# Transposes three steps and values four steps behind the scores in a fused attention and FFN kernel

## The reference

```python
x = x + 0.5 * ffn(layernorm(x))
x = x + attention(layernorm(x))
x = x + 0.5 * ffn(layernorm(x))

# attention: 16 heads of 64
h = silu(x @ W1.T + b1) @ W2.T + b2
q, k, v = split(h @ Wg.T + bg)
dots = q @ k.T * 64 ** -0.5
dots = where(j >= i + 64, -inf, dots)      # token i sees j < i + 64
out = softmax(dots) @ v
return out.reshape(b, n, 1024) @ Wo.T + bo
# ffn: silu(x wg) * (x wu) @ wd, hidden 384, weights from integers
```

## Time and profile before

| | |
|---|---|
| median of 3 runs | 1632.81 us (1631.20 to 1634.49) |
| profiled execution, time | 1628.43 us |
| its span | 1626.6 us |
| TensorE busy | 1439.0 us, 88% |
| GpSimd busy | 990.7 us, 61% |
| VectorE busy | 970.6 us, 60% |
| ScalarE busy | 776.3 us, 48% |
| mean granted TensorE clock | 0.976 of full |

### The profile page before, as it was taken

How to read it: one execution, slowest core, us unless ns; L and a number is a source line. 1 busy time by engine, 2 the same in 40 slices (tenths; PEclk the granted TensorE clock), 3 DMA queues, 4 the chain that set the end, 5 groups by cost and what they waited for, 6 DMA issues and landing times.

```text
span 1626.6 us, 38540 instructions
## 1 busy us (share of the span) xinstructions
PE 1439.0 (88%) x13330; PEld 1113.7 (68%) x13330; DVE 970.6 (60%) x1886; ACT 776.3 (48%) x1827; POOL 990.7 (61%) x592
## 2 busy tenths in 40 slices
PE   4767999999999999999999999999999999998676
PEld 3543777777777777777777777777777777777566
DVE  5653666666666666566666656666666656665444
ACT  2323555555555455554555555555555455454332
POOL 2231767677666667666676766677666666667410
PEclk9995999999999999999999999999999999999978
DMA  3100000000000000000000000000000000000000
GB/s 96 36 0 18 19 19 19 18 18 18 18 18 18 13 5 18 18 18 18 18 18 18 18 18 18 18 18 18 18 18 18 18 1 17 18 0 1 1 26 26
DMA packets 30571, 29.42 MB, mean 18 GB/s; under 512 B 6993, under 2 KB 25298, under 8 KB 30546
## 3 DMA queue, kind: packets, MB, share of 16 engines
q1 hardware_dynamic: 30546, 29.09, 5.9%
HBM read 8.07 MB, written 2.10 MB: 6 GB/s over the span
## 4 chain that ended last, share of the span: by engine, by line
PE 55%; issue 17%; DVE 13%; POOL 7%; ACT 6%; DVEq 1%; DMA 1%; ACTq 0%; POOLq 0%; SPq 0%
PE banks L773 16%; PE banks L754 15%; PE banks L789 8%; PE banks L719 6%; POOL probs L324 6%; ACT probs L389 5%; DVE probst L549 4%; DVE negmax L537 4%; PE banks L655 4%; PE banks L742 2%; PE banks L723 2%; DVE hidden L492 1%; PE banks L734 1%; POOL rstd_ln L295 1%; DVE xn_ln L478 1%
## 5 line engine op out<-in xcount | busy, mean ns | idle before, releaser
L324 POOL TENSOR_SCALAR probs<-probs,recips 128x704 f32<-128x704 f32 (+7 forms) x512 | 947.6, 1864 | 452.5 <-DVE recips L542 452.5
L537 DVE TENSOR_REDUCE negmax<-banks 128x1 f32<-128x704 f32 (+7 forms) x512 | 392.6, 808 | 129.8 <-PE banks L754 129.8
L773 PE MATMUL banks<-ident,probs 128*128 128x128 f32 x2752 | 391.4, 281 | 43.2 <-DVE probst L549 22.6
L397 ACT ACTIVATE probst<-banks 128x512 f32<-128x512 f32 (+1 forms) x320 | 177.4, 555 | 516.2 <-PE banks L773 516.2
L389 ACT ACTIVATE probs<-banks,negmax 128x704 f32<-128x704 f32 (+7 forms) x512 | 397.2, 785 | 44.5 <-DVE negmax L537 44.5
L773 PEld LDWEIGHTS banks<-ident,probs 128*128 128x128 f32 x2752 | 293.2, 141 | 130.3 <-issue 69.3
L549 DVE COPY probst<-banks 128x512 f32<-128x512 f32 (+1 forms) x416 | 276.6, 665 | 171.8 <-PE banks L773 169.8
L789 PE MATMUL banks<-probst,vs 128*64 128x128 f32 x5504 | 357.0, 277 | 0.8 <-ACT probst L397 0.8
L789 PEld LDWEIGHTS banks<-probst,vs 128*64 128x64 f32 x5504 | 295.3, 137 | 37.6 <-issue 22.5
L754 PE MATMUL banks<-kt,qt 64*128 64x512 f32 (+4 forms) x2496 | 298.3, 365 | 3.1 <-issue 3.1
L754 PEld LDWEIGHTS banks<-kt,qt 64*128 64x128 f32 x2496 | 206.0, 186 | 50.5 <-issue 5.8
(11 more groups left out here) (58 smaller groups left out, 881.1 us busy)
## 6 DMA issues: line engine op xcount, KB each, us to landing
hslot<-h_sb SPq DMA_DIRECT2D x32, 512.0 KB, 3.2
wslot<-in_wqkvt SPq DMA_DIRECT2D x32, 128.0 KB, 3.0
wslot<-wq_sb SPq DMA_DIRECT2D x32, 64.0 KB, 2.6
y<-xres SPq DMA_DIRECT2D x8, 256.0 KB, 2.3
wo_sb<-in_wot SPq DMA_DIRECT2D x1, 512.0 KB
wq_sb<-in_wqkvt SPq DMA_DIRECT2D x1, 512.0 KB
bslot<-bqk_sb SPq DMA_DIRECT2D x32, 1.0 KB, 1.9
iload<-in_wgatet SPq DMA_DIRECT2D x1, 192.0 KB, 2.4
```

Source lines behind the costliest of these rows:

```text
L324: nc.gpsimd.tensor_scalar(here, here, recips[:, c, h:h + 1], None, ALU.mult).then_inc(normed.sem, 1)
L397: nc.scalar.activation(probst[c % 2][:, 4 * g:4 * g + w, :].rearrange("p t q -> p (t q)"), banks[:, TRANSPOSED[g % 2], 0:w * P], ACT.Copy) ...
L537: nc.vector.tensor_reduce(negmax[:, c, h:h + 1], src, AX.X, ALU.max, negate=True).then_inc(maxed.sem, 1)
L773: last = nc.tensor.transpose(banks[:, TRANSPOSED[g % 2], (t - 4 * g) * P:(t - 4 * g + 1) * P], probs[c, h][:, kb * P:(kb + 1) * P], ident[:])
```

## The change

`T_LAG` goes from 2 to 3 and `PV_LAG` from 3 to 4. In step 0 the transposes are now those of step 5's tile of the turn before and the values those of step 4's.

`JOBS` is spread anew. The k and q jobs go to steps 4 to 7. v0 and v1 go to steps 1 and 3 and are now those of the turn itself, no longer of the next. An output product o1 now is that of the turn before. Where a step has two jobs (4: o3, k0; 6: o0, k1) the first is an output.

On TensorE a step is now: scores, values, transposes of groups 0 and 1, the first job, groups 2 and 3, the other jobs, masks of the next step. On ScalarE the exponentials come first, the copy of group 1 behind them. On VectorE the reciprocal stands ahead of all jobs and of the copy of group 2. `evict` is the first or second part of a step's jobs there.

Ahead of the first turn v0 and v1 aren't projected any more; behind the last one the drain has four steps instead of three, and three outputs instead of two.

```diff
--- before.py
+++ after.py
@@ -53,13 +53,15 @@
     width = [min(c * P + P + WINDOW, N) for c in range(STEPS)]
     blocks = [-(-w // P) for w in width]
     groups = [-(-2 * n // 4) for n in blocks]
-    T_LAG, PV_LAG = 2, 3
+    T_LAG, PV_LAG = 3, 4
     HEADS = "AB"
     SCORE = (0, 2)
     TRANSPOSED = (4, 5)
     ATTEND = 6
     MISC = 7
-    JOBS = {0: ["k0"], 1: ["o2", "q0"], 2: ["k1"], 3: ["o3", "q1"], 4: ["v0"], 5: ["o0"], 6: ["v1"], 7: ["o1"]}
+    JOBS = {0: ["o1"], 1: ["v0"], 2: ["o2"], 3: ["v1"], 4: ["o3", "k0"], 5: ["q0"], 6: ["o0", "k1"], 7: ["q1"]}
     JOB_ORDER = [(c, job) for c in range(STEPS) for job in JOBS[c]]
     T_BANK = {"ln1": 1, "ln2": 7}
...
@@ -214,9 +216,12 @@
             return (i, c - lag) if c >= lag else (i - 1, c - lag + STEPS)
-        def job_turn(job, c, i):
-            return i + 1 if job[0] in "kqv" else i - 1 if job in ("o2", "o3") else i
+        def job_turn(job, i):
+            return i + 1 if job[0] in "kq" else i - 1 if job in ("o1", "o2", "o3") else i
+        def runs(job, carry, more):
+            return more if job[0] in "kq" else carry or job[0] == "v" or job == "o0"
         block = ctx.enter_context(nc.Block())
...
@@ -403,23 +408,21 @@
                 act.wait_ge(wo_done.sem, wo_done.after(f"o{c // 2}", i - 1))
                 nc.scalar.activation(attn[:, c, :], banks[:, ATTEND, 0:P], ACT.Copy).then_inc(attn_out.sem, 1)
-            def step(c, i, r, carry=True, here=True, more=True):
+            def step(c, i, r, carry=True, more=True):
                 ti, tc = back(i, c, T_LAG)
                 ai, ac = back(i, c, PV_LAG)
-                turning = c < STEPS + T_LAG and (carry or c >= T_LAG)
+                turning = carry or c >= T_LAG
+                exps(c, i)
                 if turning and groups[tc] > 1:
                     take(tc, 1, ti)
-                if here:
-                    exps(c, i)
                 if carry or c >= PV_LAG:
                     attention_out(ac, ai)
                 if turning and groups[tc] > 3:
                     take(tc, 3, ti)
-                if more:
-                    for job in JOBS[c]:
-                        if job[0] in "kq":
-                            queries_keys(job, i + 1, 1 - r)
+                for job in JOBS[c]:
+                    if job[0] in "kq" and more:
+                        queries_keys(job, i + 1, 1 - r)
             for name in qk_high.events:
                 queries_keys(name, 0, 0)
...
@@ -578,24 +580,29 @@
                 ti, tc = back(i, c, T_LAG)
                 turning = carry or c >= T_LAG
                 row_max(c, i)
-                if turning:
+                if turning and groups[tc] > 0:
                     take(tc, 0, ti)
-                for job in JOBS[c]:
-                    if job[0] == "o" and (carry or job in ("o0", "o1")):
-                        add_output(job, job_turn(job, c, i))
+                invert(c, i)
+                for job in JOBS[c][:1]:
+                    evict(job, i, r, carry, more)
                 if turning and groups[tc] > 2:
                     take(tc, 2, ti)
-                invert(c, i)
-                for job in JOBS[c]:
-                    if job[0] == "v" and more:
-                        values(job, i + 1, 1 - r)
-                    if job[0] in "kq" and more:
-                        queries_keys_low(job, i + 1, 1 - r)
+                for job in JOBS[c][1:]:
+                    evict(job, i, r, carry, more)
+            def evict(job, i, r, carry, more):
+                if not runs(job, carry, more):
+                    return
+                if job[0] == "o":
+                    add_output(job, job_turn(job, i))
+                elif job[0] == "v":
+                    values(job, i, r)
+                else:
+                    queries_keys_low(job, i + 1, 1 - r)
             for name in qk_done.events:
                 queries_keys_low(name, 0, 0)
-            values("v0", 0, 0)
-            values("v1", 0, 0)
             for c in range(STEPS):
                 step(c, 0, 0, carry=False)
             with dve.Fori(0, TURNS // 2 - 1) as i2:
...
@@ -608,9 +615,10 @@
             for c in range(T_LAG):
                 ti, tc = back(TURNS, c, T_LAG)
                 take(tc, 0, ti)
-                take(tc, 2, ti)
-            add_output("o2", TURNS - 1)
-            add_output("o3", TURNS - 1)
+                if groups[tc] > 2:
+                    take(tc, 2, ti)
+            for name in ("o1", "o2", "o3"):
+                add_output(name, TURNS - 1)
             dve.wait_ge(wo_added.sem, wo_added.after("o3", TURNS - 1))
             statistics(pd, "ln1", 0, 0)
...
@@ -776,8 +784,8 @@
             def attend(c, i, r):
-                if c == 0:
-                    pe.wait_ge(v_done.sem, v_done.after("v1", i))
+                pe.wait_ge(v_done.sem, v_done.after("v0" if blocks[c] <= 4 else "v1", i))
                 n, s = back(i, c, 1)
                 pe.wait_ge(attn_out.sem, attn_out.after(s, n))
                 for e in range(2):
...
@@ -801,35 +809,29 @@
                 ai, ac = back(i, c, PV_LAG)
                 turning, attending = carry or c >= T_LAG, carry or c >= PV_LAG
-                def runs(job):
-                    return more if job[0] in "kqv" else carry or job in ("o0", "o1")
                 def do(job):
-                    if not runs(job):
+                    if not runs(job, carry, more):
                         return
                     k = JOB_ORDER.index((c, job))
-                    earlier = [(s, name, i) for s, name in JOB_ORDER[:k] if runs(name)]
-                    s, name, t = earlier[-1] if earlier else (*JOB_ORDER[-1], i - 1)
-                    misc_read(name, job_turn(name, s, t))
-                    n = job_turn(job, c, i)
-                    if job[0] in "kqv":
-                        project(job, n, 1 - r)
+                    earlier = [(name, i) for _, name in JOB_ORDER[:k] if runs(name, carry, more)]
+                    name, t = earlier[-1] if earlier else (JOB_ORDER[-1][1], i - 1)
+                    misc_read(name, job_turn(name, t))
+                    n = job_turn(job, i)
+                    if job[0] == "o":
+                        output(job, n)
                     else:
-                        output(job, n)
+                        project(job, n, r if job[0] == "v" else 1 - r)
                 score(c, i, r)
-                if turning:
-                    turns_of(tc, ti, (0, 1))
-                for job in JOBS[c]:
-                    if job[0] == "o":
-                        do(job)
                 if attending:
                     attend(ac, ai, r if c >= PV_LAG else 1 - r)
                 if turning:
+                    turns_of(tc, ti, (0, 1))
+                do(JOBS[c][0])
+                if turning:
                     turns_of(tc, ti, (2, 3))
-                for job in JOBS[c]:
-                    if job[0] != "o":
-                        do(job)
+                for job in JOBS[c][1:]:
+                    do(job)
                 if not (final and c == STEPS - 1):
                     n, s = (i, c + 1) if c + 1 < STEPS else (i + 1, 0)
                     masks(s, n)
...
@@ -838,7 +840,7 @@
             pe.wait_ge(pa.x1.sem, pa.x1.after("x", CHUNKS - 1))
             pe.wait_ge(zeroed, 2 * sum(width[c] < blocks[c] * P for c in range(STEPS)))
             last = None
-            for name in proj.events:
+            for name in ("k0", "q0", "k1", "q1"):
                 if last:
                     misc_read(last, 0)
                 project(name, 0, 0)
...
@@ -862,6 +864,8 @@
                 attend(ac, ai, 1)
                 if c < T_LAG:
                     turns_of(tc, ti, (2, 3))
+            misc_read("o0", TURNS - 1)
+            output("o1", TURNS - 1)
             misc_read("o1", TURNS - 1)
             output("o2", TURNS - 1)
             misc_read("o2", TURNS - 1)
```

More of the change, by code:

```diff
@@ L435, in _ @@
             for c in range(PV_LAG):
-                tail_step = c
                 ti, tc = back(TURNS, c, T_LAG)
@@ L441, in _ @@
                 attention_out(ac, ai)
-                if c < T_LAG:
+                if c < T_LAG and groups[tc] > 3:
                     take(tc, 3, ti)
```

## The result

The changed kernel takes 1759.47 us (median of 4 runs, 1756.98 to 1769.16) against 1632.38 us for the kernel before (4 runs). The ratio is 1.079, 95% interval 1.0745 to 1.0831. It is slower, as forecast, but by 127 us and not by 37, and lies above the range.

What follows compares the result with a forecast made beforehand. No engine is full; each step costs the longer of TensorE's blocks and the scores-maxima-exponentials-masks loop, plus other waits before the next scores. Turns +42 and ends -5.3 gave +37, so 1670 us, range 1640 to 1700.

Steps and rivals of the forecast that it cites:

- Steps 0 to 3, TensorE's blocks: Steps 0 to 3 of a turn: TensorE's own blocks decide, together 19.7 us against 21.1 before.
- The loop of steps 4 to 7 gets shorter: Scores, maxima, exponentials, masks: with exponentials ahead of ScalarE's copy, steps 4 to 7 take 19.7 us against 21.9.
- The output addition behind the reciprocal: Steps 4 and 6: k waits for VectorE's late addition; steps become 5.7 and 6.9 us, +3.1 a turn.
- q1, then the scores: End of step 7: next turn's scores wait for q1's low part; step 7 costs 7.4 us, +1.9 a turn.
- full clock for the waits it had found: TensorE's granted clock stays at 1.00 although its longest wait inside a turn becomes about 2.1 us.
- half clock for step 0: Rival: after each wait step 0's blocks run at half clock, some 3.5 us a turn more, 1775; chance 0.03.
- The ends: Start, turn 0 and last turn with drain: -5.7, -1.8 and +2.2 us, together -5.3.
- the walk of undisturbed turns: Turns 1 to 30, summed through their eight steps: 44.4 us a turn against 43.0, +42 us over 30.

Runs made afterwards that it cites:

- the last run: Changed kernel, jobs redistributed, 135 semaphore increments early on TensorE, VectorE's output additions ahead of the reciprocal, group 2's copy too in steps 6 and 7: 1596.71 us.
- shift 148: Changed kernel with 148 semaphore increments more at the start of TensorE's program: 1730.62 us.
- 147 (spread table): Changed kernel with k0 in step 0, q0 in 2, k1 in 5, q1 in 6, o0 in 7, plus 147 semaphore increments between TensorE's first projections: 1623.94 us.
- shift_before: Kernel before the change with 140 semaphore increments more at the start of TensorE's program: 1727.40 us, ratio 1.0575.
- filled wait: Changed kernel with the mask matmuls ahead of step 0's scores written 16 times, covering TensorE's wait for q1's low part: 1764.70 us.

## Why the prediction was right in direction and wrong in size

- **Steps 0 to 3, TensorE's blocks: right.** 19.7 forecast, 19.8 as the shortest.
- **The loop of steps 4 to 7 gets shorter: right.** Where nothing is added, steps 4 and 5 are 4.27 and 4.74 (4.2 and 4.72 forecast), and steps 6 and 7 reach 5.28 and 5.57 in the last run.
- **The output addition behind the reciprocal: right, a little too cheap.** Step 4 is 6.06 and not 5.7. From reciprocal to addition it takes 0.28 (I had 0.10), from the addition's end to k0 0.15 (0.05).
- **q1, then the scores: right.** 7.36 for 7.4.
- **The step that failed: full clock for the waits it had found.** It rested on one row, where TensorE waited 2.08 in the drain and its clock stayed. Inside the turns step 0 ran partly at half clock in 22 of 30: in all 14 behind a branch, where TensorE had waited 3.3 to 3.7, and in 8 of the other 16, where it had waited 1.73 for q1. By the step table over the turns, with the fetch taken out (run with shift 148), it costs 46.03 less 44.88, the sum of a turn's common full-clock steps: 1.15 a turn, 34 us. The rival "half clock for step 0" had the mechanism right and a chance of 0.03; its 3.5 us a turn were too many, since only the values and the first transposes run slowly and not behind each wait. That its 1775 lies near the 1759 measured is chance, as fetch and ends aren't in it. Why a wait of 1.73 is followed by half clock in one turn and not in the next stays open. The Trainium skill's TensorE: Matmul & The Clock Gate, section HAM oscillation, describes the array back at half rate behind every wait between bursts of matmuls, in a kernel whose waits were about twice as long as this one. The waits behind the branches agree, 14 of 14; at 1.73 it was 8 of 16.
- **What was in no sum and no rival: where the loop body lies in TensorE's program.** The prediction put it at nothing without a reason. It is 31 us of turns here, shown by shift 148. The profile before had the row (15 transfers), and I didn't ask what would change it.
- **The ends: wrong by 12 us.** I forecast -5.3 and they came to +6.7. The first scores start 1.4 earlier instead of 5.7: the first projection starts 4.4 later than before, in a part that wasn't changed; from 87.8 to that projection the granted clock was 0.79, where it had been 0.89. Why, no run tells. Turn 0 is 38.7 instead of 35.4; 1.9 of that is its step 0, which takes 4.0, with a table load on ScalarE, as it did before, and not 2.1. The last turn with its drain is about 60.7 instead of 57.5; its step 0 ran at half clock.

Together, against the span's +128.6: the walk of undisturbed turns 30 x (44.88 - 43.02) = 56, half clock 34, the fetch 31, the ends 6.7; that is 128. It adds up by construction, since clock and fetch are differences between the same three turns (44.88, 46.03, 47.08). These are from different runs, whose waits fall differently, so each part is good to some 5 us. Of the 92 us that the forecast of +37 was short, the undersized walk (44.4 for 44.88) is 14, the clock 34, the fetch 31 and the ends 12.

As a mechanism of this kernel the fetch reads so. The 141 transfers hold 16 KB each, and by the packets' times 126 are nine for each of the 14 passes back. TensorE's body is 1701 instructions before and 1721 after, two for each matmul pass. It is brought in anew in the changed kernel, unshifted or shifted by 67 or 110, in the kernel before shifted by 140, and in all runs with a changed table, order or masks and no shift. It isn't in the kernel before and in the changed one with 148, 147 (spread table) or 135 increments. This fits one rule: in pieces of 256 instructions the body may touch seven, not eight. The second stop, which moved by 40 instructions when the shift changed by 43, fits edges of pieces that stand still while the program moves over them. The Trainium skill's Runtime: NRT & Kernel Launch, section Instruction fetch mechanics, has the 16 KB pieces of 256 instructions, 128 KB of them for TensorE; the transfers' size agrees. It also says that a taken branch must fetch when its target lies outside a window of two pieces. For TensorE the runs decide otherwise: the kernel before came back 14 times over a body of nearly seven pieces without a transfer. That seven is the limit is inferred from transfers, and no run measured it by itself: open.

## What to carry to other kernels

When code is added to, taken from or moved ahead of a large hardware loop, look at the number of instruction transfers in both profiles before explaining anything else; here 140 harmless instructions ahead of the loop cost one kernel 5.8%, and 147 gave another back 3.5%. A wait that a walk finds on TensorE in every turn has a second price, for the matmuls behind it at half clock, and one row without it is too little to leave it out. And of two jobs through one bank, the release of the first must not stand behind an instruction that waits for another engine.

## What the runs showed of the hardware

- The same loop body of TensorE, moved by 140 instructions: 15 transfers and 43.0 us a turn, or 141 transfers and 45.9 us a turn.
- Behind a branch to code that had to be brought in, TensorE's next matmul started 3.3 to 3.8 us after its last one though no semaphore held it (shift_before, 14 passes); where nothing had to be brought in, 0.2 (before).
- With 110 increments ahead TensorE stopped a second time behind such a branch, one matmul on, for 2.25 to 2.95 us in all 14 passes.
- Semaphore increments on TensorE follow each other every 0.15 us. With 148 of them its first matmul started at 25.98 us instead of 17.66, its first scores 6.3 us later; most of their 22 us lay under the wait for the first input.
- Values of step 0, 24 matmuls: 1.53 us at full clock. Behind a wait of 3.3 us or more they took 1.95 to 2.83 in the changed kernel, behind a wait of 1.73 us 1.79 to 2.72 in 8 of 16 turns and 1.53 in the others. After a filled wait they took 1.53 in all 15 cases.
